# A vision block on one core: one loop for all heads in the transformer attention, f32 products by image and head triple, image blocks first, a mixture of experts in two phases

## The chip, the cores and the metric

The kernel runs on one core of a Trainium2 chip. A core has TensorE (PE in the rows; its loads of the stationary operand are shown apart as PEld), VectorE (DVE), ScalarE (ACT), GpSimd (POOL) and SyncE (SP), which only issues transfers here. The time is that of the device in microseconds; lower is better. Three runs of the kernel before took 524.59, 520.01 and 513.32 us, median 520.01. The execution that the profile shows took 514.25 us, of which 512.4 us are the span from the first instruction to the last.

## The reference

The input is 32 images as 36 patches of 768 numbers; all in all 1152 tokens of width 192.

```
h = x_patches @ W.T + b                                  # tokenizer: 1152 x 768 @ 768 x 192
xm, ref = h[:22], h[22:]                                 # 22 images, 10 reference images
m = 0.5 + 0.5*tanh(25*(c - 0.5)); c from cosines of a small gelu net of xm and ref
x = xm * m
3 times: q, v = x @ qv_w; attn = q k_ref' * s; attn = attn attn'; o = attn v (mean over refs)
         x = layernorm(x @ proj_w + proj_b, g, b)        # "diffuser"
h = layernorm(h + concat(m*x + (1-m)*xm, ref))
# transformer layer
x = h + softmax(q k' / 4) v @ proj_w + proj_b            # q, k, v of layernorm(h); 12 heads of 16,
                                                         # 36 tokens of one image attend to each other
xn = layernorm(x)
top 2 of 8 logits xn @ gate_w, softmax over the two
y = sum of the two experts: gelu(xn @ w1[e] + b1[e]) @ w2[e] + b2[e]     # 192 -> 768 -> 192
out = layernorm(h + x + y)
```

## The kernel before, in words

Tokens are worked on in 11 blocks of three images (108 rows, NT = 11); the last holds 72. Blocks 0 to 7 hold images of the diffuser (MT = 8; the last of them also holds the first references). Each engine has its own program, written out by hand as Python loops, and the order within it is the order of the text; semaphores (`S[...]`) tie the engines together. Nothing is scheduled by a planner. The stages are:

- **Tokenizer** (time 5 to 37 us). Per block six f32 matmuls, the bias by DVE (L955), two transposes (L400), a copy by ACT.
- **Prologue** (37 to 70 us). With all blocks there: the small net (three gelu passes), the reference keys, their Gram matrix, the cosines, the mask. ACT also issues here the nine transfers that fill the sort buffer `srt_dram` in memory with zeros (L746), ahead of the copies of the keys (L753).
- **Diffuser.** NI = 24 steps (three rounds of eight blocks) in a software pipeline: step i makes the queries and values of block i (`wq`, `wqv`), the products `rm` of step i-1, and the projection (`wpa`) of step i-5, whose result went through memory (`scratch`) to change its layout. Five more turns, 24 to 28, drain the pipeline. Beside this, ACT and POOL split 27 pieces of weights into a 16-bit high part (L731) and a bf16 low part (L1286): 24 for the experts, three for attention. Up to two pieces come in a turn, one on most; the last at turn 26. SP issues every transfer, in order.
- **Attention** (17 turns, about 220 to 369 us). A block passes through a pipeline of turns: features q and k as split products (three 16-bit matmuls for one f32 product), scores over the 108 x 108 tokens of three images with a barrier value between images, maximum by DVE (L1099), exponential by ACT (L850, one for each head), 12 transposes (L584), a split of the probabilities, 36 matmuls of 17 columns for the heads, a projection as a split product, residual sum, layer norm (statistics on DVE, the root on POOL by `pow`, L1261), logits, top 2, rank within the expert. Blocks go in the order 0 to 10, so that block 0 has to wait for the drained diffuser.
- **Routing.** Once all blocks are chosen, DVE makes a table of 25 tiles of 128 rows (L1162 to L1187); rows go to the sorted buffer by indirect transfers (L1291) and come back by tile (L366).
- **Mixture** (389 to 489 us). 25 tiles, each of 36 + 18 split products, a gelu in three pieces (ACT L901), a cast and a subtraction in two pieces (DVE L1206, L1208). POOL writes the scaled diagonals `dg` here (L1332).
- **End.** The results are read back by token, summed by PE with the diagonals of the gates, normed and stored.

The helpers `mm` (L395) and `turn` (L400) record nearly all matmuls and transposes, so these are told apart by the names of their operands.

## Time and profile before

| what | us |
|---|---|
| median of 3 runs (513.32 to 524.59) | 520.01 |
| profiled execution | 514.25 |
| its span | 512.4 |
| PE busy | 401.5 (78%) |
| DVE, POOL, ACT busy | 288.8, 233.3, 227.5 |
| mean granted clock of TensorE | 0.817 of 2.4 GHz |

A busy PE is not a PE at its peak: a matmul's end is modelled, and at the lower clock level (0.5, that is 1.2 GHz) the same work is busy for nearly twice as long. One f32 matmul is two records.

### The profile page before, as it was taken

The page shows a single profiled execution, that of the slowest core. Times are in us where ns is not written, and L with a number is a line of the kernel's source. Part 1 is how long each engine was busy: PE and PEld are TensorE (multiplying, and loading weights), DVE is VectorE, ACT ScalarE, POOL GpSimd, SP SyncE. Part 2 cuts the span into 40 slices and gives each one's busy share as a digit, 9 for nine tenths or more (in the row PEclk, how much of TensorE's full clock was granted, in tenths as well). Part 3 has the DMA queues.
Part 4 walks back from the last instruction along what each step waited for, and adds up shares of the span by engine and source line. Part 5 has one row for each costly group of instructions (what it writes and reads, how often), then busy time and mean ns, then how long its engine had stood idle before and what let it go on. Part 6 is the DMA issues. An engine that isn't in the chain of part 4 may idle for free.

```text
span 512.4 us, 12626 instructions
## 1 busy us (share of the span) xinstructions
PE 401.5 (78%) x4370; PEld 341.2 (67%) x4370; DVE 288.8 (56%) x843; ACT 227.5 (44%) x636; POOL 233.3 (46%) x358
## 2 busy tenths in 40 slices
PE   3996376889999965276999889876407999999974
PEld 3984354546766644175889789766406998989964
DVE  1111132234545567568988687653553888888823
ACT  1121313467777753157775555441104544445403
POOL 1000001366666656835475644435432666666524
PEclk9999567979999995559897676655556999999988
DMA  8706915447566652000000000000253776667233
GB/s 255 264 0 222 297 41 115 111 91 193 141 146 147 146 105 59 0 3 1 3 3 3 14 16 14 14 14 28 63 224 109 267 256 229 246 227 281 98 103 106
DMA packets 59725, 59.62 MB, mean 116 GB/s; under 512 B 36843, under 2 KB 46197, under 8 KB 58896
## 3 DMA queue, kind: packets, MB, share of 16 engines
q1 hardware_dynamic: 56400, 48.10, 31.3%
q10 hardware_dynamic: 1008, 7.15, 4.3%
q0 software_dynamic: 2256, 3.57, 2.2%
q8 instruction: 37, 0.61, 0.5%
q14 instruction: 24, 0.20, 0.1%
HBM read 25.55 MB, written 14.33 MB: 78 GB/s over the span
## 4 chain that ended last, share of the span: by engine, by line
PE 61%; DVE 11%; issue 6%; POOL 6%; ACT 5%; DMA 4%; ACTq 3%; SPq 3%; POOLq 0%; DVEq 0%
PE wide L395 27%; PE bank L395 27%; PE bank L400 4%; ACTq L746 3%; ACT xT L850 3%; PE bank L584 1%; POOL rstd L1261 1%; DVE xs L1017 1%; PE bank L660 1%; DMA bdm<-in_bdm 1%; PE wide L584 1%; DMA xT<-in_w 1%; DVE xT L1132 1%; POOL srt_dram L1291 1%; SPq L313 1%
## 5 line engine op out<-in xcount | busy, mean ns | idle before, releaser
L395 PEld LDWEIGHTS bank<-xT 108*32 108x32 f32 (+4 forms) x629 | 24.3, 144 | 36.7 <-issue 24.6
L395 PE MATMUL bank<-xT 108*32 108x96 f32 (+4 forms) x629 | 32.4, 263 | 19.5 <-ACT xT L731 11.4
L764 ACT ACTIVATE xT<-bank,gains 96x128 f32<-96x128 f32 (+1 forms) x72 | 29.0, 461 | 36.0 <-PE bank L660 36.0
L1291 POOL DMA_INDIRECT srt_dram<-row,dst x22 | 22.9, 1039 | 45.3 <-DVE dst L1089 39.6
L1337 POOL DMA_INDIRECT y_dram<-qkbm,ydst x25 | 26.0, 1038 | 35.7 <-DVE ydst L1214 27.1
L731 ACT ACTIVATE xT<-wide 108x288 f32<-108x288 f32 (+1 forms) x70 | 26.2, 410 | 35.9 <-PE wide L395 19.7
L395 PE MATMUL bank<-wqv,xTs 128*108 128x384 f32 x96 | 38.7, 529 | 4.4 <-DVE xT L1032 4.3
L1286 POOL TENSOR_TENSOR wqkl<-xT,wqkh 96x768 bf16<-96x768 f32 x2 | 3.2, 1632 | 84.9 <-ACT wqkh L731 84.9
L395 PE MATMUL wide<-xT 108*108 108x17 f16 (+4 forms) x511 | 39.4, 223 | 0.0
L395 PE MATMUL wide<-w2h,xs 128*128 x300 | 39.1, 246 | 0.0
L395 PEld LDWEIGHTS wide<-xT 108*108 108x108 f16 (+4 forms) x511 | 37.2, 161 | 0.0
L395 PE MATMUL wide<-w2l,xs 128*128 x150 | 36.9, 246 | 0.0
L1208 DVE TENSOR_TENSOR xs<-xT,xs 128x384 bf16<-128x384 f32 x50 | 35.4, 709 | 1.7
L1206 DVE CAST xs<-xT 128x384 f16<-128x384 f32 x50 | 28.8, 577 | 11.3 <-ACT xT L901 9.9
L850 ACT ACTIVATE xT<-bank,nmax 108x108 f32<-108x108 f32 x99 | 25.1, 369 | 22.7 <-DVE nmax L1099 22.7
L395 PE MATMUL bank<-tokw,xT 128*108 128x192 f32 x132 | 28.2, 372 | 8.0 <-DMA xT<-in_xT 5.3
L395 PE MATMUL wide<-xT,wqkh 96*128 96x108 f16 (+1 forms) x264 | 30.1, 261 | 4.2 <-DVE xT L1053 4.2
L1260 POOL TENSOR_SCALAR veps<-mv 108x1 f32<-108x1 f32 x46 | 10.8, 235 | 48.9 <-DVE mv L934 48.3
L395 PE MATMUL bank<-wpa,ocT 128*108 128x192 f32 x96 | 25.1, 391 | 7.3 <-DVE yb L1029 4.8
L395 PEld LDWEIGHTS bank<-tokw,xT 128*108 128x108 f32 x132 | 24.8, 202 | 9.0 <-DMA tokw<-in_tokw 5.2
L395 PEld LDWEIGHTS wide<-xT,wqkh 96*128 96x128 f16 x264 | 26.7, 128 | 4.8 <-ACT xT L731 3.8
L395 PE MATMUL wide<-xT,wqkl 96*128 96x108 f16 x132 | 29.3, 261 | 0.0
(257 smaller groups left out, 1240.2 us busy)
## 6 DMA issues: line engine op xcount, KB each, us to landing
srt_dram<-row ACTq DMA_DIRECT2D x8, 800.2 KB, 10.4
xT<-in_xT SPq DMA_DIRECT2D x11, 324.0 KB
tokw<-w1h SPq DMA_DIRECT2D x9, 384.0 KB
e1T<-w1l SPq DMA_DIRECT2D x9, 384.0 KB
hT<-in_w SPq DMA_DIRECT2D x8, 384.0 KB, 3.5
xT<-in_w SPq DMA_DIRECT2D x8, 384.0 KB, 3.6
vecs<-w1h SPq DMA_DIRECT2D x8, 384.0 KB
wqv<-w1l SPq DMA_DIRECT2D x8, 384.0 KB
```

The lines of the kernel that those rows point to most:

```text
L395: return nc.tensor.matmul(o, l, r, start=start, stop=stop)
L400: last = nc.tensor.transpose(o[:, f, :], i[:, f * HF:(f + 1) * HF], ident[0:T, 0:T])
L584: last = nc.tensor.transpose(bank[1 + r][0:T, g * T:(g + 1) * T], prob[:, 3 * r + g, :], ident[0:T, 0:T])
L731: return nc.scalar.activation(o, i, ACT.Copy)
L746: nc.scalar.dma_start(srt_dram[z * 96:(z + n) * 96].rearrange("(p r) w -> p (r w)", p=96), blank[:, 0:n * W]).then_inc(S["zeroed"], 16)
L764: last = nc.scalar.activation(o[:, f], i[:, f], ACT.Identity, scale=gains[:, which, 0, f:f + 1], bias=gains[:, which, 1, f:f + 1])
L850: last = nc.scalar.activation(prob[:, hh, :], bank[1 + r][0:T, g * T:(g + 1) * T], ACT.Exp, bias=nmax[:, hh:hh + 1])
L1206: V.tensor_copy(high, hidf[:, i % 2, cols]).then_inc(S["hidh_ready"], 1)
L1208: V.tensor_tensor(hidl[:, i % 2, o].rearrange("p j n -> p (j n)"), hidf[:, i % 2, cols], high, ALU.subtract).then_inc(S["hidl_ready"], 1)
L1260: link(G.tensor_scalar(ve, var, EPS, None, ALU.add))
L1291: G.indirect_dma_start(srt_dram, bass.IndirectOffsetOnAxis(dst[:, t, k:k + 1], 0), row[:, t, 0:W], None, bounds_check=EXP * CAP - 1, oob_i ...
L1337: G.indirect_dma_start(y_dram, bass.IndirectOffsetOnAxis(ydst[:, q:q + 1], 0), ysb[:, q % YB], None, bounds_check=2 * NTOK - 1, oob_is_err ...
```

## The change

What it does, by stage:

- **Tokenizer and prologue are one loop** (`for s in range(NT + 2)`). The reference blocks 7 to 10 come first (`TILES`), and the net, the keys, the Gram matrix and the mask of the first three blocks are worked out between the matmuls of later blocks. Only two constants (`FIRST`) are awaited ahead of the second block. The square root of the norms goes to POOL by `pow`. The zero fill is issued by SP, behind the inputs.
- **Diffuser.** The 24 steps stay. Attention has no more pieces to split; the 24 pieces of the experts are dealt two to a step in steps 0 to 4, one each in 5 to 10 and 14 to 21. The first layer norm of the three blocks of references alone (`begun`) stands in steps 11 to 13. The last five turns are inside the attention loop.
- **Attention** is one loop of 11 turns. All its products are f32. The order of blocks is `ATT` = 8, 9, 10, 0 to 7. DVE spreads the queries of a block into block-diagonal form by head triple (`qbd`, 108 columns: three heads of 36 tokens), so that scores are 12 matmuls of 36 columns against the 36 keys of one image, on 64 rows each. The probabilities are 108 x 432; maximum, addition and exponential are one instruction each; four transposes; four matmuls of 147 columns with values masked by image (`vj`), whose last columns give the sums; DVE masks and scales (`om`), and six matmuls with `dup` give the columns for the projection. Biases ride on a row of ones. ACT applies the layer norms.
- **Routing is spread** over the turns: block a is chosen in turn a+3 and its rows are sent at once.
- **Mixture in two phases.** Out of the first eight blocks of `ATT` come at least FULL = 5 full tiles. Their table is made in turn 10, and these tiles start while blocks 8 to 10 of the order go through the rest of attention and routing. The table of the other 20 tiles is made by DVE beside tile 2.
- **ACT** takes from DVE the cast of the hidden layer's high part (both halves in tiles 0 to 4, the second half afterwards), and from POOL the diagonals of the gates, in tiles 8 to 18. `RING` is 4 in place of 8.

```diff
+TILES = [*range(MT - 1, NT), *range(MT - 1)]
-RING, YB = 8, 3
+RING, YB = 4, 3
+AHEAD = 3
+SOON = NT - 3
+REFS_AT = NT
+ATT = [*range(MT, NT), *range(MT)]
+FULL = (2 * sum(min(T, B * N - t * T) for t in ATT[:SOON]) - EXP * (P - 1)) // P
...
-            return 3 + q // 2 if q < 6 else q
+            return q // 2 if q < 10 else q - 5 if q < 16 else q - 2
...
+            sp.wait_ge(S["zeros_ready"], 1)
+            blank = row[0:96].rearrange("p t w -> p (t w)")
+            for z, n in ZEROS:
+                sp.dma_start(srt_dram[z * 96:(z + n) * 96].rearrange("(p r) w -> p (r w)", p=96),
+                             blank[:, 0:n * W]).then_inc(S["zeroed"], 16)
...
+            sp.wait_ge(S["place_ready"], 1)
+            sp.wait_ge(S["row_stored"], 16 * 2 * SOON)
+            sorted_rows(0)
+            sorted_rows(1)
+            sp.wait_ge(S["exp_ready"], 1)
+            expert_weights(0)
+            expert_weights(1)
+            sorted_rows(2)
+            expert_weights(2)
             for i in range(WB, NTILE):
+                if i == FULL:
+                    sp.wait_ge(S["place_ready"], 2)
+                    sp.wait_ge(S["row_stored2"], 16 * 2 * (NT - SOON))
                 sorted_rows(i)
...
-                    for g in range(3):
-                        for r in range(4):
-                            rows = slice(32 * r, 32 * r + 32)
-                            last = split_mm(bank[1 + r][0:T, g * T:(g + 1) * T], [(qkh[rows, 0, g], qkl[rows, 0, g])],
-                                            [(qkh[rows, 1, g], qkl[rows, 1, g])])
+                    for u in range(2):
+                        for j in range(JB):
+                            for a in range(2):
+                                rows = slice(64 * a, 64 * a + 64)
+                                last = mm(wide[0:T, a, (u * JB + j) * N:(u * JB + j + 1) * N], qbd[rows, u, j], kT[rows, u, j * N:(j + 1) * N])
...
+            def mixed(a):
+                pe.wait_ge(S["pT_ready"], a + 1)
+                pe.wait_ge(S["av_ready"], a + 1)
+                pe.wait_ge(S["y_read"], min(NI - 4 + a, NI))
+                if a >= 1:
+                    pe.wait_ge(S["om_ready"], a)
+                for g in range(HG):
+                    last = mm(wide[0:T, 2 + g // 2, g % 2 * OG:g % 2 * OG + VW], pT[:, g * T:(g + 1) * T], vj[:, a % 2, g, :])
+                last.then_inc(S["ao_psum"], 1)
...
+            def high_of(i, a):
+                act.wait_ge(S["hid_ready"], HJ // 2 * i + 2 + a)
...
+                copy(hidh[:, i % 2, 3 * a:3 * a + 3].rearrange("p j n -> p (j n)"),
+                     hidf[:, i % 2, a * 3 * P:(a + 1) * 3 * P]).then_inc(S["hidh2_ready" if a else "hidh_ready"], 1)
```

How this moves instructions, at three places. First ACT, from the prologue to the first diffuser step. Before (`e1T` is the net's gelu, `srt_dram<-row` the zero fill, the copies `xT<-bank` behind it the reference keys, `th` the mask, `xTs` the transposed block):

```order
L742 ACTIVATE e1T<-wide,fc1b 48x432 x2
L742 ACTIVATE e1T<-wide,fc1b 48x324
L746 DMA srt_dram<-row 96x2134 x8
L746 DMA srt_dram<-row 96x1552
L753 ACTIVATE xT<-bank,rowm 108x192
L731 ACTIVATE xT<-bank 108x192 x3
L757 ACT_TABLE_LOAD
L757 ACTIVATE nrm<-nrm 108x11
L759 ACT_TABLE_LOAD
L759 ACTIVATE th<-cosm 108x8
L731 ACTIVATE xTs<-bank 96x216 x2
```

Now, from the fifth block on (the keys go to `xs`):

```order
L870 ACTIVATE e1T<-wide,fc1b 48x108
L854 ACTIVATE hT<-bank 96x2x108
L878 ACTIVATE xs<-bank 108x192
...
L854 ACTIVATE hT<-bank 96x2x108
L864 ACTIVATE th<-cosm 108x3
L870 ACTIVATE e1T<-wide,fc1b 48x108
L854 ACTIVATE xTs<-bank 96x216 x2
L943 ACTIVATE h<-h,mask 108x192
L854 ACTIVATE w1h<-xT 128x768
```

The nine transfers have left ACT, the keys are copied between the blocks, and no table is loaded between the last gelu and the mask.

Second PE, one turn of attention. Before, from the head products of a block to those of the next (`xT<-` 108x17 are the heads, 108x108 the scores, `wqkh`/`wqkl` the features, the L584 rows the transposes of the probabilities):

```order
L395 MATMUL wide<-xT 108x17 x36
L395 MATMUL wide<-wvph,xT 108x192
L395 MATMUL wide<-wvpl,xT 108x192
...
L395 MATMUL bank<-xT 108x108 x9
L395 MATMUL wide<-xT 108x108 x3
...
L395 MATMUL wide<-xT,wqkh 128x108 x2
L395 MATMUL wide<-xT,wqkl 128x108
...
L584 MATMUL bank<-ident,xT 108x108 x9
L584 MATMUL wide<-ident,xT 108x108 x3
```

Now one turn from turn 5 on, with its waits (108x147 are the heads, 108x36 the scores, `amask` is `dup`):

```order
L433 MATMUL bank<-xTs,wqk 128x108 [waits aq_ready,aoT_ready,qT_ready,x1T_ready]
L433 MATMUL bank<-xTs,wqk 128x108 x3
L641 MATMUL bank<-ident,xT 108x108 [waits taken_ready,pT_ready,p_ready]
L641 MATMUL bank<-ident,xT 108x108 x3
...
L433 MATMUL wide<-xT 108x147 [waits y_read,om_ready,av_ready,pT_ready]
L433 MATMUL wide<-xT 108x147 x3
L433 MATMUL wide<-xT 108x36 [waits e_ready,o_ready,res_ready,ak_ready,aq_ready]
L433 MATMUL wide<-xT 108x36 x11
...
L433 MATMUL bank<-amask,xT 96x36 [waits aoT_ready,aq_ready,om_ready]
L433 MATMUL bank<-amask,xT 96x36 x5
...
L433 MATMUL wide<-wvo,xT 108x192 [waits res_ready,e_ready,aoT_ready]
```

The 36 + 36 + 36 split matmuls of features, scores and heads are 8 + 12 + 4 of f32, 12 transposes are 4, and six matmuls are new.

Third PE, where the mixture starts (L750 are the transposes of sorted rows, `row` those of a block's router rows):

```order
L750 MATMUL bank<-ident,xT 96x128 [waits srt_in0,chosen_ready]
L750 MATMUL bank<-ident,xT 96x128
L438 MATMUL bank<-ident,row 96x108 [waits xn_ready]
L438 MATMUL bank<-ident,row 96x108
L433 MATMUL wide<-chosen,rank 108x8 [waits chosen_ready,e_ready]
L433 MATMUL wide<-chosen,rank 128x8
```

The rows of tile 0 are transposed here before the last three blocks have their ranks; before, tile 0 stood behind all of them.

## Rows read from the trace of the kernel before

**Rows 1.** The page's granted clock in 40 slices of 12.8 us, in tenths.

```profile
PEclk9999567979999995559897676655556999999988
```

**Rows 2.** Windows by stage: from:to, us, busy of each engine, granted clock, DMA share, GB/s.

```profile
104.00:177.00 73.00, 72.01 (x693) 49.11 (x694) 35.94 (x97) 51.84 (x133) 48.86 (x65) 0.96 0.63 145
233.00:354.00 121.00, 106.28 (x1428) 97.17 (x1428) 90.84 (x302) 68.75 (x239) 60.53 (x116) 0.73 0.04 10
354.00:387.00 33.00, 8.86 (x42) 7.58 (x42) 15.16 (x75) 2.86 (x8) 13.53 (x17) 0.50 0.37 126
387.00:489.00 102.00, 97.93 (x1394) 93.19 (x1395) 83.31 (x199) 49.55 (x126) 60.80 (x70) 0.97 0.59 212
```

**Rows 3.** Timeline, tokenizer and prologue: start, us, engine, line, operation, [idle before, releaser].

```profile
12.19 4.18 PE L395 MATMUL bank<-tokw,xT 128*108 128x192 f32 x12 [2.76 <-DMA bdm<-in_bdm]
34.46 2.12 PE L395 MATMUL bank<-tokw,xT 128*108 128x192 f32 x12
41.59 15.10 ACTq L746 DMA_DIRECT2D srt_dram<-row  x9
69.61 1.65 PE L395 MATMUL bank<-xTs,wq 128*96 128x108 f32 x8
```

**Rows 4.** Timeline, diffuser steps and their drained end.

```profile
101.20 0.84 ACT L731 ACTIVATE w1h<-xT 128x768 f16<-128x768 f32 x1 [4.27 <-DMA xT<-in_w]
177.30 0.91 PE L395 MATMUL bank<-xTs,wq 128*96 128x108 f32 x8
182.85 0.91 PE L395 MATMUL bank<-xTs,wq 128*96 128x108 f32 x8
190.84 2.05 DVE L1017 TENSOR_TENSOR xs<-xs,vecs 108x192 f32<-108x192 f32 x1 [1.94 <-ACT xs L782]
```

**Rows 5.** Timeline, first of the maxima of attention turns 0, 2, 4 and 10.

```profile
226.49 1.30 DVE L1099 TENSOR_REDUCE nmax<-bank 108x3 f32<-108x324 f32 x3 [0.62 <-PE wide L395]
243.47 1.29 DVE L1099 TENSOR_REDUCE nmax<-bank 108x3 f32<-108x324 f32 x3
260.33 1.28 DVE L1099 TENSOR_REDUCE nmax<-bank 108x3 f32<-108x324 f32 x3
332.41 1.29 DVE L1099 TENSOR_REDUCE nmax<-bank 108x3 f32<-108x324 f32 x3
```

**Rows 6.** Timeline, matmuls at either clock level.

```profile
262.39 1.33 PE L584 MATMUL bank<-ident,xT 108*108 108x108 f32 x9
265.01 0.46 PE L395 MATMUL wide<-gate,hT 96*108 96x8 f32 x4
287.41 0.76 PE L395 MATMUL wide<-gate,hT 96*108 96x8 f32 x4
171.12 0.90 PE L395 MATMUL bank<-wpa,ocT 128*108 128x192 f32 x4
171.95 0.63 PE L395 MATMUL wide<-rm,xT 32*108 32x96 f32 x12
```

**Rows 7.** Groups by form, whole span: line, engine, operation, shapes, count, busy, mean ns, idle.

```profile
L850 ACT ACTIVATE xT<-wide,nmax 108x108 f32<-108x108 f32 x33 | 9.8, 415 | 0.0
L782 ACT ACTIVATE xs<-yb,shift,rstd 108x192 f32<-108x192 f32 x24 | 13.1, 547 | 33.4 <-POOL shift L1264 33.3
L764 ACT ACTIVATE xTs<-bank,gains 96x108 f32<-96x108 f32 x32 | 12.3, 443 | 0.0
L1206 DVE CAST xs<-xT 128x384 f16<-128x384 f32 x50 | 28.8, 577 | 11.3 <-ACT xT L901 9.9 <-issue 1.3
```

**Rows 8.** Chain of waits, routing and first tile: start, us, what.

```profile
384.01 2.19 DMA xT<-srt_dram
389.05 2.72 PE bank L395 x24
```

**Rows 9.** Timeline, the last sending of rows, and PE's first matmul behind the mixture.

```profile
376.13 0.99 POOL L1291 DMA_INDIRECT srt_dram<-row,dst  x1 [0.30 <-issue]
489.34 1.48 PE L395 MATMUL bank<-h,ident 108*108 108x192 f32 x8
```

1535 lines of the change are left out of this document (870 added, 665 removed).

## The prediction

> **What bounds the kernel now.** I read the windows by stage first, then the timeline at the seams between stages. PE is the bound in two stages and in neither of the others. In the steady diffuser PE is busy for 72.01 of 73 us, in the mixture for 97.93 of 102 [rows 2]; the change leaves the work of both on PE as it is. In attention it is busy for 106.28 of 121 us, but at a granted clock of 0.73 [rows 1, 2], that is partly at 1.2 and partly at 2.4 GHz. In routing it is busy for 8.86 of 33 us: a chain of small instructions and waits. So what can be won lies in the prologue, at the drained end of the diffuser, in attention and in routing, and each is read at its seams: the diffuser's first `wq` at 69.61, its last at 182.85, the first maximum at 226.49, the one of turn 10 at 332.41, the first hidden matmul at 389.05, the first matmul behind the mixture at 489.34 [rows 3, 4, 5, 8, 9]. The sum goes from seam to seam against the profiled execution: 512.4 us of span and 1.85 around it, 514.25. The median of the runs shown is 520.01, 1.1% above it, and the three spread over 2.2%, so that the forecast for a median has a percent of doubt from there alone.
>
> **Tokenizer and prologue, new end 51 (before 69.61).** Block 1 started at 12.19 because its matmuls stood behind all early constants (2.76 us idle) [rows 3]. Now only two are ahead of it; the others are some 570 KB, and at the 245 GB/s of this stretch 2 us: start at about 10.5. A block's six matmuls take 2.12 us at the full clock and 4.18 at the low one [rows 3]; ten blocks 21, and 3 for the ramp of the clock as before. Between them PE now also does, per block, two transposes, two gelu matmuls of 108 columns and one of 24, and altogether eight key matmuls, sixteen of the Gram and `wqg` kind and four for the cosines. The nearest rows are eight records of 108 columns in 0.91 us and four of 8 columns in 0.46 [rows 4, 6]: a record is 0.09 to 0.1 us. That makes about 1.0 us a block, 11 in all, and 5 for the rest. 10.5 + 21 + 3 + 16 = 50.5, so 51. It replaces 32 us between the tokenizer's last matmul (34.46 + 2.12) and 69.61, of which 15.1 were ACT issuing the zero fill with the keys behind it [rows 3]. SP issues the fill now, while nothing behind it in its queue is due for another 15 us: at nothing, and if the fill held back the first pieces, their wait (as below) would cost about 4.
>
> **Diffuser, new last `wq` at 161 (before 182.85).** A steady step is 4.39 us, and 17 of them with one stall of 1.1 us led up to 182.85; so the sixth step began at 107 and the first six took 37.5 us, 11 more than steady. Part of that was ACT standing for pieces (4.27 us idle for one) with the step's copies behind them [rows 4]. Now two pieces come in each of steps 0 to 4, loaded a step ahead, the second behind the copies; but ACT also has the second half of the mask and a table load. I take half the excess off and a little back: 33 for the first six. Then 17 × 4.39 = 75, and 2 for the three double roots on POOL in steps 11 to 13. 51 + 33 + 75 + 2 = 161. That the second half of the late steps has no pieces on POOL also ends stalls such as the 2.05 us of DVE's multiplication at 190.84 [rows 4].
>
> **The seam to attention, new first maximum at 172.5 (before 226.49).** Before, 43.6 us lay between the last `wq` and the first maximum: five drained turns at the low clock and the split of attention's first block. Now the first attention block is a reference block that waits for nothing, and the drained turns lie within the loop. What is left is a step (4.4) and the features, the last products and the scores of turn 0, about 7: 11.5. Turns 0 to 4 carry one transposition, projection, bias, moments and normalisation each, priced below.
>
> **Attention, ten periods of 12.1 us (before 105.9 us, 10.6 each).** At the full clock two periods took 260.33 - 243.47, 8.43 each; the mean over ten is 1.26 times that [rows 5]. The new PE work of a turn, at the full clock: features 16 records 1.8 (eight are 0.91 [rows 4]); four transposes 0.6 (nine are 1.33 [rows 6]); values and projection 0.9 each (four records of 192 columns [rows 6]); heads eight records of 147 columns 1.0; six `dup` products, 12 records, 1.2 (four records are 0.46 [rows 6]); four transposes of 96 rows 0.7; logits and ranks 0.8. Scores have no row of their own: 24 records of 36 columns on alternate halves of the rows. One bound is 1.2 us (12 records on three row groups are 0.63 [rows 6]), the other 2.4 (no overlap, 0.1 each). I take 1.2, since the alternation is of the former kind. The sum is 9.1 and, with ends that overlap the next group taken off, 8.3; in turns 0 to 4 about 0.5 more. At the low clock the same rows are 1.65 to 1.8 times as long (0.76 for 0.46, 1.65 for 0.91 [rows 3, 4, 6]): 15.
>
> Here a rule can be laid beside the rows. At the low clock four short f32 records go from 0.46 to 0.76 us [rows 6]. The Trainium skill (TensorE: Matmul & The Clock Gate, LDWEIGHTS) puts a load of P columns at P / 1.2 ns, whatever the clock, 90 ns here. By it the 36 short records would not slow down, and a low-clock turn would be about 2 us shorter; the sum would be 435. The measured records decide. A rule against the change: the same skill (FP8 and Floating Point Precision, TensorE Precision Notes) has true FP32 in four passes, where the split products take three. By that alone the features, values and projection would cost 1 us more a turn, and attention would lose 10 us; the dropped transposes and the merged heads are what the rows set against it.
>
> A turn has a chain too. From ACT's copy of the keys to the next one: four row norms of 0.55, three masked copies of the values at 0.4, the heads' copy 0.35, the exponential over 432 columns (0.415 at 108 [rows 7]; I take 0.65), two affine copies 0.8: 5.2 us. Then PE's queries 0.9, transposes 0.6, ACT's copy 0.6, keys and their copy: 8.0, and with ten handoffs of 0.15 to 0.2 us 9.6. The chain is thus a little above PE's sum at the full clock, and below it at the low one. Between turns at either level I take the mix of before: 9.6 × 1.26 = 12.1. The bounds are 9.6 and 15. New maximum of turn 10: 172.5 + 121 = 293.5. So attention itself is forecast to be no faster than before, rather slower; the gain is in what lies around it.
>
> **Routing, new first hidden matmul at 309.5, 16 us later (before 56.6).** Before, 12.9 us went by from the last sending of rows (376.13) through the transfer (384.01) to 389.05 [rows 8, 9]; in front lay six more turns and a table. Now the eighth block is ranked in turn 10 itself: maximum and sum 1.3, `send_to` 1.2, POOL's two sendings 2.3, the way of before 12 from there, less 1 as the table is no longer ahead of it. About 16. DVE's 18 table instructions stand ahead of block 9's residual; 3.7 us, hidden by that transfer.
>
> **Mixture and end.** The work on PE stays: 489.34 - 389.05 = 100.3. Added: the last three blocks' residual, norm, logits and ranks between tiles 0 to 2, where PE, DVE and ACT wait for each other. I take 6 for these and 3 for two table loads around ACT's exponential in tile 5. The half of a cast that ACT takes over is about 0.55 us (DVE's was 0.577 [rows 7]); two of them, 0.8 for the columns and 1.15 for three gelus are 3.1 of a tile's 3.93, and 3.3 with the diagonals but one cast. At nothing, covered by PE; if ACT became the bound it would be 0.3 × 20 = 6. The end is 23.1 as before.
>
> **Sum.** 309.5 + 100.3 + 9 + 23.1 + 1.85 = 443.7, so **443 us**, 14% under the profiled execution.
>
> **The rivals.**
> - *Full clock.* The clock was 0.97 in the mixture and 0.96 in the steady diffuser [rows 2]; f32 products stream for longer. Then a turn is its chain, 9.6: 443 - 25 = 418. Against it: the chain leaves PE idle for 1.3 us of each turn, and before, at the full clock, PE was as dense and still lost it.
> - *Low clock throughout.* Before, from turn 6 on most slices show 0.5 to 0.7 [rows 1]. Then a turn is 15: 443 + 29 = 472.
> - *The two phases don't start early.* SP's queue is in order, and tile 0 needs rows, table and pr_psum of the last block; if the first five tiles wait for the whole routing chain, or starve behind it, some 20 us come back: 463.
> - *Slower than before.* One mechanism: short f32 products with 108 stationary columns whose loads don't overlap, at the low clock, with ACT's chain not beside them but behind. Scores 4.3 in place of 2.3, `dup` products 2.4, and ACT's 5.2 us exposed: 15 + 2.3 + 5.2 = 22.5, and DVE's 1.3 us ahead of them: 24. Ten periods add 119: 562. It decides from a period of 20.5 us on. Against it: score products on several row groups do overlap in this trace [rows 6].
>
> **Chances.** Forecast case (430 to 457) 0.50; full clock 0.20; low clock 0.17; phases not early 0.10; slower 0.02; 0.01 for about no change. The range runs from the full-clock case with an early prologue to the low-clock case: 412 to 476, the likeliest case's own 430 to 457. A difference of 2% is about what a measurement of this kernel can tell from none; faster by more 0.97, within 0.01, slower 0.02.
>
> **What would show it.** The first `wq` near 51 with no zero fill on ACT; the step still 4.4; the first maximum 11 to 12 us behind the last `wq`; maxima 9.6 to 15 apart according to the granted clock; the first hidden matmul 16 behind the last maximum, before the last three blocks' ranks; tiles of 3.93 from tile 3 on. It would be wrong if turns were over 15 at the full clock, or tiles stretched by ACT.

## The result, and the profile after

The changed kernel took 409.89 us (median of four runs, 404.55 to 414.34) against 520.68 for the kernel before: a ratio of 0.786 with an interval of 0.761 to 0.811. A second measurement, of six runs beside eleven of the kernel before, gave 413.98 us and 0.798 (0.793 to 0.803). Both ratios go by the faster runs of each kernel, since some executions of either are a per cent or two slower at a lower granted clock. It is faster, by about the amount of the case "full clock" (418), not by that of the forecast (443); at 409.9 it lies two microseconds under the range of 412 to 476.

The profiled execution took 414.34 us, of which 412.5 are the span. The page's granted clock, which answers to [rows 1]:

```profile
PEclk9999988999999998669999699995989999999969
```

The digits of 5 that filled the drained diffuser and the routing of the kernel before are gone, but for one slice. Next the windows of the changed kernel, from:to, us, busy of PE, PEld, DVE, ACT and POOL, granted clock, DMA share, GB/s; they answer to [rows 2]:

```profile
89.00:160.00 71.00, 68.41 (x679) 47.69 (x675) 37.93 (x102) 48.38 (x129) 48.09 (x87) 0.99 0.47 95
174.67:269.55 94.88, 90.44 (x825) 83.33 (x826) 67.55 (x223) 51.93 (x136) 57.02 (x137) 0.93 0.07 23
269.55:284.00 14.45, 11.15 (x73) 10.14 (x74) 9.48 (x43) 7.67 (x18) 4.68 (x9) 0.78 0.27 98
284.00:388.52 104.52, 98.52 (x1410) 96.54 (x1411) 77.32 (x213) 69.95 (x179) 48.22 (x56) 0.97 0.63 225
```

The second row is attention from the first maximum to that of turn 10: ten periods in 94.9 us at a clock of 0.93, where 121 were forecast. The seams, from the timeline (start, us, engine, line, operation, what ended the wait before it); they answer to [rows 3, 4, 5, 9]:

```profile
52.21 1.60 PE L433 MATMUL bank<-xTs,wq 128*96 128x108 f32 x8
159.29 1.65 PE L433 MATMUL bank<-xTs,wq 128*96 128x108 f32 x8
174.67 0.61 DVE L1402 TENSOR_REDUCE nmax<-wide 108x12 f32<-108x432 f32 x1 [6.06 <-PE wide L433]
269.55 0.61 DVE L1402 TENSOR_REDUCE nmax<-wide 108x12 f32<-108x432 f32 x1
284.00 0.27 PE L433 MATMUL bank<-xh,tokw 128*128 128x128 f16 x1 [0.47 <-DMA e1T<-w1l]
388.52 1.48 PE L433 MATMUL bank<-h,ident 108*108 108x192 f32 x8
```

| from seam to seam | before | forecast | after |
|---|---|---|---|
| to the first `wq` | 69.6 | 51 | 52.2 |
| to the last `wq` | 113.2 | 110 | 107.1 |
| to the first maximum | 43.6 | 11.5 | 15.4 |
| ten periods of attention | 105.9 | 121 | 94.9 |
| to the first hidden matmul | 56.6 | 16 | 14.4 |
| to the first final matmul | 100.3 | 109.3 | 104.5 |
| to the end | 23.1 | 23.1 | 24.0 |

Six of the seven seams were within 5 us, and their errors cancel to -3.3. Attention alone was off by 26.1. So the question for the experiments was why a turn takes 9.5 us and not 12.1, and what the factor 1.26 of the kernel before had been. In a row of undisturbed turns the maxima stand 8.8 us apart:

```profile
234.33 0.61 DVE L1402 TENSOR_REDUCE nmax<-wide 108x12 f32<-108x432 f32 x1 [0.17 <-PE wide L433]
243.13 0.61 DVE L1402 TENSOR_REDUCE nmax<-wide 108x12 f32<-108x432 f32 x1
251.94 0.61 DVE L1402 TENSOR_REDUCE nmax<-wide 108x12 f32<-108x432 f32 x1
```

The window between the last two of them, at the full clock:

```profile
243.13:251.94 8.81, 8.55 (x85) 7.81 (x86) 6.49 (x24) 5.43 (x15) 6.44 (x16) 1.00 0.07 21
```

### The profile page after: what moved, and what is told of

It reads as the page before. It is cut to its first block, busy times and chain, and to the rows that moved or that the text cites. A ratio compares the mean times of both kernels' runs of the same rounds, so it can differ in the third digit from the quotient of the medians.

```text
span 412.5 us, 11162 instructions
## 1 busy us (share of the span) xinstructions
PE 373.7 (91%) x3714; PEld 320.6 (78%) x3714; DVE 230.3 (56%) x703; ACT 225.4 (55%) x574; POOL 196.9 (48%) x339
## 4 chain that ended last, share of the span: by engine, by line
PE 72%; POOL 6%; DVE 6%; issue 6%; DMA 4%; ACT 3%; SPq 1%; ACTq 0%; POOLq 0%; DVEq 0%
PE bank L433 38%; PE wide L433 28%; PE bank L438 4%; POOL rstd L1536 2%; ACT xTs L885 1%; DMA srt_dram<-row,dst 1%; PE bank L750 1%; DVE xT L1261 1%; DMA xT<-in_xT 1%; PE bank L641 1%; POOL shift L1539 1%; POOL srt_dram L1575 1%; DMA e1T<-w1l 1%; POOL veps L1535 1%; POOL veps L1545 1%
## 5 line engine op out<-in xcount | busy, mean ns | idle before, releaser
L1619 POOL DMA_INDIRECT y_dram<-ysb,ydst x25 | 24.8, 993 | 49.1 <-PE wide L433 18.3
L854 ACT ACTIVATE xT<-bank 108x192 f32<-108x192 f32 (+3 forms) x57 | 21.0, 368 | 30.5 <-PE bank L433 17.7
L433 PE MATMUL bank<-xTs,wqk 128*128 128x108 f32 x176 | 28.5, 313 | 4.7 <-ACT xTs L885 2.8
L433 PE MATMUL wide<-xT 64*108 64x36 f32 (+2 forms) x368 | 32.2, 283 | 0.2 <-ACT xT L854 0.2
L433 PEld LDWEIGHTS wide<-xT 64*108 64x108 f32 (+1 forms) x368 | 29.8, 185 | 2.7 <-issue 2.3
L1575 POOL DMA_INDIRECT srt_dram<-row,dst x22 | 23.1, 1049 | 17.7 <-DVE dst L1317 9.8
L433 PEld LDWEIGHTS bank<-xTs,wqk 128*128 128x128 f32 x176 | 25.0, 219 | 8.2 <-ACT xTs L885 6.0
L433 PEld LDWEIGHTS bank<-xT 108*32 108x32 f32 (+2 forms) x316 | 14.2, 122 | 17.7 <-issue 17.3
L1536 POOL TENSOR_TENSOR rstd<-veps,nhalf 108x1 f32<-108x1 f32 x46 | 26.1, 567 | 3.8
L885 ACT ACTIVATE xT<-bank,gains 96x128 f32<-96x128 f32 x50 | 20.0, 448 | 14.3 <-PE bank L750 14.3
L433 PEld LDWEIGHTS wide<-w2h,xs 128*128 128x128 f16 (+1 forms) x300 | 26.4, 98 | 0.0
L854 ACT ACTIVATE xT<-wide 108x288 f32<-108x288 f32 x48 | 16.9, 405 | 14.7 <-PE wide L433 14.5
```

Of the source, the lines that this page charges most:

```text
L433: return nc.tensor.matmul(o, l, r, start=start, stop=stop)
L854: return nc.scalar.activation(o, i, ACT.Copy)
L885: last = nc.scalar.activation(o[:, f], i[:, f], ACT.Identity, scale=gains[:, which, 0, f:f + 1], bias=gains[:, which, 1, f:f + 1])
L1536: last = G.tensor_tensor(rstd[0:rows, k], ve, nhalf[0:rows], ALU.pow)
L1575: G.indirect_dma_start(srt_dram, bass.IndirectOffsetOnAxis(dst[:, t, k:k + 1], 0), row[:, t, 0:W], None, bounds_check=EXP * CAP - 1, oob_i ...
L1619: G.indirect_dma_start(y_dram, bass.IndirectOffsetOnAxis(ydst[:, q:q + 1], 0), ysb[:, q % YB], None, bounds_check=2 * NTOK - 1, oob_is_err ...
```

## Experiments on the changed kernel: TensorE, the clock and the gaps

Times of the whole are single runs unless said otherwise, and they spread by some us. So I read attention in its own ten periods (from the first maximum to that of turn 10). In six profiles whose attention code is that of the changed kernel these took 92.6 to 97.0 us, so that a difference of 4 us is not told from none.

**Scores twice.**

```diff
-                    for u in range(2):
+                    for again in range(2):
+                        for u in range(2):
```

> In the changed kernel, ten periods between maxima took 94.9 us, the undisturbed ones 8.8 each, at a granted clock of 0.93; TensorE was busy for 90.6 of 95 us. Here the twelve score products of each turn are made twice (the first set is overwritten), 24 more f32 records of 36 columns. If TensorE bounds the turn, all that the second set takes is added; the first set's rows show 2.3 us: period 11.1, ten of them 118, the whole some 25 us longer. If the chain through ACT and DVE is the bound, as the prediction had it for the full clock (9.6 us against 8.3 of TensorE), the second set first fills slack and the ten periods grow by 10 us or less. Both theories of the clock leave it at 0.93 or above here, since the added work is f32 and leaves no gap.

Measured: 419.75 us, ten periods 99.7 in place of 94.9, and no dip in the clock (windows of this run):

```profile
172.00:271.70 99.70, 95.22 (x1065) 88.81 (x1066) 67.60 (x224) 53.23 (x136) 57.31 (x137) 1.00 0.07 22
```

The 2.3 us expected were a misreading: that row holds the 147-column products too. Two rows show the size of the added set. The first is the changed kernel, the second this run; both begin with the same products:

```profile
240.65 2.43 PE L433 MATMUL wide<-xT 108*108 108x147 f32 x32
```

```profile
237.74 3.57 PE L433 MATMUL wide<-xT 108*108 108x147 f32 x56
```

24 more records are 1.14 us, 11.4 in ten turns. Without its one long turn (13.2 in place of 8.8) the changed kernel would have had 90.5; this run's 99.7 are 9.2 more. So about 0.8 of what is added to TensorE shows. TensorE's idle time stays at 4.4 to 4.5 us in either window (94.88 less 90.44, 99.70 less 95.22), so the added work fills no slack: TensorE bounds the turn, with the chain through ACT and DVE close behind. The forecast had it the other way round: 8.3 for TensorE, 9.6 for the chain. TensorE's 8.8 less a wait of 0.2 is 8.6, the 8.3 were nearly right, and the chain was put too long.

**Short 16-bit products added.**

```diff
+                    for z in range(42):
+                        mm(wide[0:T, 0, 432:449], w2h[0:T, z % EXP, z % HJ, 0:T], w2h[0:T, z % EXP, z % HJ, 108:125])
```

> Ahead of each turn's scores stand 42 products of 17 columns with 16-bit operands, whose result nobody reads: of the same kind as the 36 that made the heads in the kernel before, and at the full clock about as long as the doubled scores of the run beside it (2.1 to 2.3 us a turn). Theory of gaps (the clock falls where TensorE is idle in between): no gap is added, so the clock stays at 0.93 and the ten periods take 95 + 22 = 117 us. Theory of kinds (short 16-bit products don't hold the clock, whatever the gaps): the clock of attention falls toward the 0.73 of before, and the ten periods take 135 us or more.

**A gap each turn.**

```diff
                     last.then_inc(S["s_psum"], 1)
+                    pe.wait_ge(S["e_ready"], i + 1)
```

> No work is added: in each turn TensorE waits behind the scores until DVE has taken the maximum and added it, 1.2 us and two handoffs, which makes a gap of about 1.5 us a turn, as large as the idle time per turn in attention of the kernel before (14.7 us in 121). Theory of gaps: the clock falls toward 0.73, and a period goes from 8.8 to 10.3 and then by the clock to 12 or more: ten periods 120 to 135. Theory of kinds: the clock stays at 0.9 or above, and the ten take 95 + 15 = 110. In the least case, that the gap only replaces other waits, nothing changes.

Measured: 458.34 and 454.21 us. The windows of ten periods, first of the run with short products, then of the run with the gap:

```profile
173.12:310.72 137.60, 136.67 (x1245) 132.55 (x1246) 69.30 (x223) 52.87 (x136) 56.91 (x137) 0.73 0.05 16
```

```profile
170.97:301.46 130.49, 113.15 (x824) 107.12 (x824) 69.52 (x223) 53.67 (x139) 56.59 (x137) 0.74 0.06 17
```

Each brought the clock down to the level of before, the first with TensorE hardly idle (136.67 of 137.60), the second without a single product added. Neither theory excludes the other: here the added short products and the added gaps are each enough, and the f32 work of the doubled scores kept 1.00. What it is in the short products is not shown, since the two sets differ in three things: 42 products of 17 columns in 16 bits against 24 records of 36 columns in f32. TensorE's idle time grew from 0.44 to 1.73 us a turn, and the turn by 3.6.

**GpSimd's sends later.** The one long turn of the changed kernel (221.12 to 234.33) has this behind it: ACT waited 2.63 us for a norm's shift by POOL, then TensorE stood for 1.22, and then came 8 us at 0.57. Timeline of ACT and PE, then a window, in the changed kernel:

```profile
221.81 0.55 ACT L971 ACTIVATE row<-xT,shift,rstd 108x192 f32<-108x192 f32 x1 [2.63 <-POOL shift L1539]
224.88 0.90 PE L433 MATMUL wide<-wvo,xT 128*108 128x192 f32 x4 [1.22 <-ACT xT L854]
```

```profile
226.00:234.00 8.00, 8.00 (x54) 7.68 (x56) 4.11 (x15) 2.78 (x7) 5.93 (x14) 0.57 0.03 9
```

```diff
-                if i + AHEAD >= NT:
+                if i == NT - 1:
                     send(i - 3)
...
-                if 3 <= i < NT - AHEAD:
-                    send(i - 3)
+                for a in {5: [0], 6: [1], 7: [2], 8: [3, 4], 9: [5, 6]}.get(i, []):
+                    send(a)
```

> The changed kernel, in which GpSimd sends rows in turns 5 to 10 and not from turn 3 on. In turns 3 and 4 it had three norms, a sum and two sends, 9.3 us of work without a pause, and ACT waited 2.6 us for it in turn 5; TensorE stood for 1.22 us, the clock fell to 0.57 for 8 us, and that period was 13.2 us in place of 8.8. If this was GpSimd's backlog, the long period goes, ten periods take 88 to 91 us at a clock near 1.0, and the whole gains 4 to 6 us. If the stall is of another origin it stays, and nothing is gained. The price: the last sends are 1 to 2 us later, and with them tile 0 perhaps.

Measured: 416.93 us. The long turn is gone (9.5 us in its place), so GpSimd's backlog was its cause. But another of 13.0 us stands at the end (252.1 to 265.1); the ten periods are 94.6, and the seam to the first hidden matmul is 17.3 in place of 14.4, at a clock of 0.50. Ahead of the new stall ACT's copies begin 1.45 us behind TensorE's last value product (250.49 + 0.90), and then TensorE stands for 1.67:

```profile
250.49 0.90 PE L433 MATMUL bank<-wvo,xTs 128*108 128x192 f32 x4
252.84 1.05 ACT L1038 ACTIVATE xT<-bank,rowm 108x192 f32<-108x192 f32 x3 [3.73 <-PE bank L433]
254.83 0.90 PE L433 MATMUL wide<-wvo,xT 128*108 128x192 f32 x4 [1.67 <-ACT xT L854]
```

GpSimd issues its four sends in just this time (248.50 to 253.45), but no wait in the program ties ACT's copies to them. So this stall stands beside the doubled sends and is not shown to come from them; moving the sends gained nothing.

## Experiments on the kernel before: what the factor 1.26 was

**Filled with f32 work, and f32 products for the heads.**

```diff
                         if a == 1:
+                            for z in range(5):
+                                last = mm(bank[6][0:T, 3 * T:4 * T], ident[0:T, 0:T], ident[0:T, 0:T])
```

> The kernel before, with five f32 transpose-sized products of 108 columns (into columns that nobody reads) behind the key features of every attention turn: 1.1 us of f32 work at the full clock, where TensorE would then have waited for the exponential. Theory of gaps: with the longest wait filled the clock of attention rises from 0.73 to 0.85 or more, and ten periods take 105.9 or less, down to 98, although there is more work. Theory of kinds: most of a turn's records are still short 16-bit ones, the clock stays near 0.73, and the ten periods take 105.9 + 10 to 15 = 116 to 121.

```diff
-                    for hh in range(HEADS):
-                        last = split_mm(bank[7][0:T, hh * (HD + 1):(hh + 1) * (HD + 1)], ...
+                    for hh in range(8):
+                        last = mm(bank[7][0:T, hh % 2 * 102:(hh % 2 + 1) * 102], rank[:, 1, 0:T], prob[:, hh, 0:102])
```

> The kernel before, in which the 36 short 16-bit products that make the heads of a block (17 columns each, 1.93 us a turn at the full clock) are left out and eight f32 products of 102 columns stand in their place (sixteen records, about 1.8 us at the full clock); so the heads are not those of the reference, the order, the waits and the length of the work are the same. Theory of kinds: the clock of attention rises from 0.77 to 0.9 or more and ten periods fall from 105.9 us to 85 to 95. Theory of gaps: nothing about the gaps has changed, the clock stays at 0.77 and the ten take 103 to 108.

Both together:

> Both edits of the kernel before at once: f32 products in place of the 36 short 16-bit ones of the heads (so the heads are not those of the reference), and the five f32 products of 108 columns behind the features. Each alone left the clock of attention at 0.82 and 0.79, with TensorE idle for 15% and 8% of it. If idle time and short products each hold the clock down, and both must go, it rises here to 0.9 or more, and ten periods take 93 to 98 us, less than the 105.9 of before although each turn has 1.1 us more work. If the clock hangs on something else (the order of stages, the chain through DVE), it stays at 0.8 and the ten take 108 to 115.

Measured: 521.64, 516.29 and 517.21 us (the kernel before 513.77, 516.35 and 512.59 beside them); ten periods 111.8, 108.1 and 106.6 at clocks of 0.79, 0.82 and 0.89. The first lies between its two expectations, the second near that of gaps, and the third is in neither: with both edits the clock rose by 0.12, and the ten periods were not shorter. Nearly 35 us of that last run, its last three turns, show why (window):

```profile
301.60:336.10 34.50, 28.48 (x375) 24.49 (x372) 24.84 (x93) 20.73 (x72) 16.68 (x24) 0.95 0.06 17
```

At a clock of 0.95 the turns are still 11.5 us long, and TensorE is idle for 6 of 34.5. Nor is it the added work that makes them long. The five added products lie in a wait: the transposes behind them still wait 0.23 us for ACT three times a turn. The f32 head products take 1.74 us at the full clock where the short ones took 1.95; in the middle turn of the three, where the clock dipped (0.57 from 318 to 322), they took 2.95:

```profile
318.23 2.95 PE L395 MATMUL wide<-xT,rank 108*108 108x102 f32 x16
330.63 1.74 PE L395 MATMUL wide<-xT,rank 108*108 108x102 f32 x16
```

The other two turns had the full clock throughout and took 11.2 and 10.8 us (windows):

```profile
301.61:312.82 11.21, 9.21 (x135) 7.99 (x132) 8.70 (x33) 7.26 (x25) 5.58 (x8) 1.00 0.06 18
325.30:336.05 10.75, 8.15 (x109) 6.67 (x105) 7.94 (x31) 6.22 (x22) 5.56 (x8) 1.00 0.06 17
```

So the late turns of the kernel before had another bound for the most part, and I formed a new theory: a ring (maxima, exponentials, transposes, heads, DVE's splits and choice, maxima).

**DVE's order changed.**

```diff
                 (behind the maxima of turn i)
+                if 0 <= i - 6 < NT:
+                    choose(i - 6)
+                if 0 <= i - 7 < NT:
+                    send_to(i - 7)
```

> The kernel before, with DVE's choice of experts and its rank arithmetic (twelve small instructions, 2.1 us) behind the next block's maxima and no longer ahead of them. In the run with both fillings the last three turns of attention had a clock of 0.95 and still took 11.5 us each, against 8.4 in the first turns, where no block is routed yet. Theory of the ring: from turn 5 on a turn is a ring (maxima, exponentials, transposes, heads, DVE's choice, maxima), and the low clock comes with TensorE's waits in it. Then the late turns lose the 2.1 us at least, down to 9.5 to 10.3 from 12.0, ten periods take 92 to 98 in place of 105.9, and the clock rises from 0.77 to 0.85 or more. Theory of the clock alone: DVE's order matters little; ten periods stay at 103 or more.

Measured: 518.42 us, ten periods 109.1, clock 0.72. It decides nothing, since the edit made a wait of its own: GpSimd's sends came ahead of the root on which DVE waits, and TensorE waits for DVE.

```profile
320.36 0.96 DVE L940 TENSOR_SCALAR row<-yb,mv,rstd 108x192 f32<-108x192 f32 x1 [2.06 <-POOL rstd L1262]
```

> The run with DVE's choice behind the maxima said nothing clear: with it GpSimd's two sends came to stand ahead of the norm's root, DVE waited 2.06 us for that root and TensorE 2.13 for DVE. Here the sends stand a turn later on GpSimd too, behind the root, so that the order of DVE is changed alone. Theory of the ring: the late turns of the kernel before come down from 12.0 us to 10.3 or less, ten periods to 92 to 98. Theory of the clock: the late turns keep 11.5 to 12, ten periods 103 or more.

> The same order, and both fillings of the kernel before (f32 products in place of the short ones of the heads, so that these are not the reference's, and five f32 products of 108 columns a turn). The fillings alone had raised the clock to 0.89, to 0.93 in the late turns, which kept 11.5 us. If ring and clock each held the late turns, only both edits free them: 9.3 us a turn, ten periods 93 to 96 at a clock of 0.95. If the choice is not what closes the ring, the late turns stay at 11.5 and the ten at 105.

Measured: 501.51 and 500.52 us (the kernel before 512.86 beside them); ten periods 99.5 at a clock of 0.79 and 97.3 at 0.96. The order alone gave 6.4 us of attention at nearly the same clock (0.77 before), nearly all of it in the three turns from 260.33 to 296.56, which took 36.2 before and 30.8 now. In the four runs with the old order these three turns took 36.2 to 39.0, so this is more than their spread. With both fillings at work the order is worth more: the same three turns take 38.5 without it and 28.3 with it. The last three turns gained nothing (35.8 before). First with the order alone, then with all three edits (windows):

```profile
288.20:323.80 35.60, 33.89 (x442) 31.53 (x440) 26.67 (x93) 21.19 (x72) 20.52 (x30) 0.70 0.07 19
```

```profile
285.20:320.70 35.50, 29.31 (x412) 26.43 (x410) 26.43 (x92) 21.18 (x72) 20.56 (x30) 0.95 0.07 19
```

35.6 us at a clock of 0.70 and 35.5 at 0.95: here the clock is worth nothing. By the rows it is GpSimd's sends that close these turns. The last send and the maxima behind it, first with the order alone, then with all three edits:

```profile
310.45 0.99 POOL L1292 DMA_INDIRECT srt_dram<-row,dst  x1 [0.31 <-issue]
311.94 1.30 DVE L1099 TENSOR_REDUCE nmax<-bank 108x3 f32<-108x324 f32 x3 [1.09 <-remote]
```

```profile
307.40 1.05 POOL L1294 DMA_INDIRECT srt_dram<-row,dst  x1 [0.31 <-issue]
308.89 1.30 DVE L1101 TENSOR_REDUCE nmax<-bank 108x3 f32<-108x324 f32 x3 [1.04 <-remote]
```

In both runs the maxima of each of the last three turns start 0.44 to 0.50 us behind the end of GpSimd's second send. From the maxima to the moments on DVE it is 5.0 us, from there through GpSimd's root, differences, sums and sends 6.3, and 0.5 more to the next maxima: 11.8, a turn, and no TensorE work lies in it. The program has no wait of the maxima for the sends, and the profile puts the end of the wait to no engine; why DVE stands there is open. And this ring comes with the edit: in the kernel before the sends ended 8.0 us or more ahead of the maxima. So for its late turns only the run with both fillings speaks.

Ten periods at the 8.43 us of the two fast ones [rows 5] would be 84.3; the kernel before had 105.9. An estimate for the 21.6 between, from the rows above: the three middle turns lost 10.9 to that pace, of which DVE's order gave back 5.4 and 3.0 are left even with it at a clock of 1.00 (28.3 less 25.3); the last three lost 10.6, of which 7.0 to 8.3 are left in turns of 10.8 to 11.2 us at the full clock. That is 15 to 17 us for waits. 5 to 6 are left for the clock, about a quarter of what I had put on it.

## Experiments on the other terms

**The drained steps ahead of attention.** The five results are made before the loop on PE, ACT, DVE and POOL, and no longer in its turns 0 to 4:

```diff
+            for k in range(5):
+                turn_result(NI - 5 + k, NI)
...
+                projection(NI - 5 + k)
```

> The changed kernel with the last five steps' results (transposition, projection, bias, moments, normalisation) taken out of attention's turns 0 to 4 and made ahead of the loop, as in the kernel before. They are a chain of about 3 us each there (two transposes 0.35, ACT's copy, projection 0.9, bias, and the next), so the first maximum comes 15 us later, and the five turns give back 1.6 us of TensorE's each, 8 in all: +5 to +9 us. If a sparse stretch ahead of attention decides about its clock, there is more: ten periods at 0.75 in place of 0.93 to 1.0, 115 us or more, +25 to +30 in all.

Measured: 426.35 us. The seam to the first maximum is 27.2 in place of 15.4, the ten periods 91.6 in place of 94.9, at the same 0.93: +8.5 by these two, inside the range (the whole is 12.0 above the profiled execution, the rest lies in other seams). The 3.3 us that the turns gave back are less than the 8 expected, and no more than profiles of one code differ by. A sparse stretch ahead of it does not decide about attention's clock. Of the 28.2 us that this seam lost, 11.8 are the folding; the rest I put on the order of blocks and what no longer has to be split, by subtraction: no run takes these apart.

**One phase.**

```diff
             sp.wait_ge(S["row_stored"], 16 * 2 * SOON)
+            sp.wait_ge(S["row_stored2"], 16 * 2 * (NT - SOON))
             sorted_rows(0)
```

with the ranks of the last three blocks and the second table ahead of tile 0 on each engine.

> The changed kernel without its early phase: all eleven blocks are ranked and sent, and both tables made, before the first tile's rows are fetched. In the changed kernel the first hidden product comes 14.4 us behind turn 10's maximum. The three last blocks' routing (a residual, a norm, a transposition, logits and ranks that wait for each other, about 4 us for each that no other work hides), the table of 20 tiles (3.7) and the transfer (8) then stand ahead of it: 30 to 34 us behind that maximum, and the mixture gets back the 4 us that it took more than before. So +12 to +16 us. If the early phase's worth is mainly that TensorE's clock doesn't fall, the mixture's first tiles show it too (+3 more). If it were hidden anyway: within 4 us of the changed kernel.

Measured: 427.28 us. The routing seam is 35.2 us in place of 14.4, the mixture 98.4 in place of 104.5: the early phase is worth 14.7 by these two seams (12.9 by the whole). The rest of the 42.2 us that the routing seam lost I put on spreading, by subtraction; no run shows it alone.

**The zero fill back on ACT.**

```diff
+            for z, n in ZEROS:
+                nc.scalar.dma_start(srt_dram[z * 96:(z + n) * 96]...
             from_turn(0)
```

> The changed kernel with the eight transfers of zeros issued by ACT behind the tokenizer's loop, ahead of the first diffuser block's columns, as before they stood ahead of the keys. An issue took ACT 1.7 us before (15.1 for nine), most of it while the inputs still came. If the price of an issue is in its queue's room, and room is short only while inputs come, eight issues cost about 0.1 to 0.4 each here: +1 to +3 us at the first query product. If the price is fixed by the 800 KB that each moves, the first query product comes 13 to 15 us later, and the whole is 13 to 15 us longer.

Measured: 428.11 us, the first `wq` at 66.98. The issues (eight of 800 KB and a smaller one), first on SP in the changed kernel, then on ACT in this run:

```profile
16.76 4.39 SPq L348 DMA_DIRECT2D srt_dram<-row  x9
```

```profile
50.91 15.17 ACTq L1004 DMA_DIRECT2D srt_dram<-row  x9
```

The same transfers cost SP 4.4 us, right behind the issues of all inputs, and ACT 15.2 at a time when SP issues only first pieces of weights: the price is not the room that the inputs take. The first `wq` comes 14.8 us later, and the whole is 13.8 above the profiled execution.

**The casts back on DVE.**

```diff
-                if i >= FULL and a == 0:
-                    V.tensor_copy(high, hidf[:, i % 2, cols]).then_inc(S["hidh_ready"], 1)
+                V.tensor_copy(high, hidf[:, i % 2, cols]).then_inc(S["hidh2_ready" if a else "hidh_ready"], 1)
```

> The changed kernel with both halves of the hidden layer's cast on DVE in all tiles, as before; ACT makes none. The prediction put the move to ACT at nothing, covered by TensorE, whose work of a tile is 3.7 to 3.9 us: the time from the first to the last hidden product stays within 2 us of 104.5. The other side: DVE's work of a tile (casts 0.58 each, subtractions 0.73 each, bias 0.36, high part 0.29, destinations 0.4) then comes to 3.7 us, and with its handoffs it, not TensorE, sets the tile: 0.1 to 0.3 us more on each of 25, +3 to +7.

Measured: 416.61 us. Tiles by their results' bias, first the changed kernel, then this run:

```profile
350.26 0.35 DVE L1497 TENSOR_TENSOR ysb<-wide,hT 128x192 f32<-128x192 f32 x1
353.94 0.35 DVE L1497 TENSOR_TENSOR ysb<-wide,hT 128x192 f32<-128x192 f32 x1
357.60 0.34 DVE L1497 TENSOR_TENSOR ysb<-wide,hT 128x192 f32<-128x192 f32 x1
```

```profile
352.07 0.35 DVE L1493 TENSOR_TENSOR ysb<-wide,hT 128x192 f32<-128x192 f32 x1
355.95 0.35 DVE L1493 TENSOR_TENSOR ysb<-wide,hT 128x192 f32<-128x192 f32 x1
359.83 0.35 DVE L1493 TENSOR_TENSOR ysb<-wide,hT 128x192 f32<-128x192 f32 x1
```

3.67 us a tile with ACT's casts in this stretch (in other profiles 3.6 and 4.0 in turn), 3.88 without, and the kernel before had 3.9. Over 14 tiles in the middle of the mixture the mean is 3.95 here and 3.77 to 3.83 in four profiles of the unchanged mixture. So the move that I put at nothing gave 0.1 to 0.2 us a tile, 2 to 4 in all. That DVE, not TensorE, set the tile before is argued from this, and fits the other side of the expectation; no wait of TensorE in the profile shows it. The mixture took 109.0 in place of 104.5, but with unchanged code it took 109.7 in another profile: the period of a tile shows this, the sum doesn't.

**Products of zeros at the start and the end; the gates' exponential by a power.**

```diff
+            for z in range(14):
+                mm(bank[7][0:T, 0:P], warm[0:T, 0:T], warm[0:T], False, False)
             for t in range(NT):
```

> The changed kernel with products of a zero tile at two places: eight ahead of the tokenizer (TensorE is idle there until 5.17 us and its first two blocks take 4.15 us each in place of 2.12) and fourteen between the start of the final sums and the arrival of the expert results (3.4 us idle, after which sixteen records take 5.42 us in place of 2.9). Theory of gaps: the first two blocks take 2.1 to 3 us each and the final sums come 2 us earlier; the whole gains 2 us at the end, and at the start up to 3, unless the tokenizer waits for its inputs anyway (DMA at 98% of its time up to 38 us), which I expect: -2 us in all. If the products don't move the clock: the end is later by the little that they overlap, 0 to +1.

```diff
-                    nc.scalar.activation(vv[:, 1, :], vv[:, 0, :], ACT.Exp).then_inc(S["gex_ready"], 1)
...
+                    link(G.memset(vv[:, 1, :], 2.718281828459045))
+                    G.tensor_tensor(vv[:, 1, :], vv[:, 1, :], vv[:, 0, :], ALU.pow).then_inc(S["gex_ready"], 1)
```

> The changed kernel with the exponential of the gates made by GpSimd as e to a power, so that ACT loads no table in the mixture. The prediction put 3 us on the two loads in tile 5 (1.28 each and their place in the gelus). Tile 5's period was 5.7 us in the changed kernel, the others' 3.7 to 4.0. If the loads are the cause, it comes down to about 4: -1.7 to -2.5 us in all. If it is the fetch of rows behind the second table (the same tile is the first of it), it stays at 5.5 and nothing is gained.

Measured: 414.78 and 413.91 us. With the zeros the end takes 22.0 us in place of 24.0, as expected (23.2 to 25.1 in other profiles without them); at the start the first block takes 2.17 us in place of 4.15, and then the second waits for its input:

```profile
5.20 2.17 PE L434 MATMUL bank<-tokw,xT 128*108 128x192 f32 x12 [0.76 <-DMA xT<-in_xT]
9.56 3.09 PE L434 MATMUL bank<-tokw,xT 128*108 128x192 f32 x12 [2.19 <-DMA xT<-in_xT]
```

With the power the slow tile takes 4.5 us in place of 5.7: the two table loads were 1.2 of my 3.

**All three mends, beside the changed kernel on the same chip, six runs each.**

> The changed kernel with three edits: GpSimd's sends later (4 to 6 us if the backlog theory holds), the exponential of the gates by a power on GpSimd (1.4 us, as the run of it alone showed in tile 5), and products of zeros while TensorE waits for the expert results at the end (2 us). Sum: 7 to 9 us less than the changed kernel on the same chip, about 2%, some 400 us.

> The changed kernel itself, as the base for the run beside it: 405 to 415 us, ten periods of attention 95 us, one of them 13 us long, the seam from turn 10's maximum to the first hidden product 14.4.

Measured: 413.55 us (409.88 to 420.68), ratio to the kernel before 0.801 (0.794 to 0.807); the changed kernel 413.98 (409.09 to 417.05), 0.798 (0.793 to 0.803). No gain, where 7 to 9 us were expected. The sends gave back in a late turn of 13.0 us and in the routing seam (17.1) what they took from turn 6; the other two should leave 3 us, and such a difference is within what these runs can tell. The changed kernel stays the fastest that was run.

The profile of the changed kernel taken here met its expectation in the seam (14.4) but not in attention: the ten periods are 96.9, and the same wait of 2.63 us for GpSimd and the same stand of TensorE (1.23) are followed by two long turns, 14.4 and 12.5 us (window):

```profile
212.56:239.48 26.92, 25.61 (x177) 24.05 (x178) 14.59 (x50) 12.43 (x32) 16.27 (x35) 0.68 0.05 15
```

That is 9.3 us more than two turns of 8.8, where the first profile lost 4.4.

## Why the prediction was wrong

The direction was right, the number was 33 us too high. By its steps:

- **Tokenizer and prologue** (51; 52.2), with ACT's 15.1 us of issues on the path: right, and shown by putting them back. (Its 245 GB/s are 262 in the stretch from 5.28 to 12.19; that changes nothing.)
- **Diffuser** (110; 107.1): right in the sum, with one row misread. The `wq` that stands 17 steps ahead of 182.85 is at 100.09 and not at 107; between it and the next one lie 11.1 us, so that 6.7 of the 11 us in excess stood in one stall and not spread over the first steps:

```profile
100.09 0.91 PE L395 MATMUL bank<-xTs,wq 128*96 128x108 f32 x8
111.17 0.91 PE L395 MATMUL bank<-xTs,wq 128*96 128x108 f32 x8
```

- **Seam to attention** (11.5; 15.4): low by 4; I had priced the features and scores of turn 0 at the full clock, and the stretch has 0.72.
- **Attention** (121; 94.9): the failed step is "Between turns at either level I take the mix of before: 9.6 × 1.26 = 12.1". The factor is the ratio of all ten periods to two fast early ones of the kernel before, and I took it for the clock because the clock was low in the late turns (the two early ones, called full clock in the prediction, had 0.90, as the window below shows). The runs on the kernel before show that most of it was waits between the engines, of DVE's order above all: by the estimate above 15 to 17 of 21.6 us. And the changed kernel shows in its place a turn of 8.8 us at a clock of 1.00, set by TensorE. What is the clock's own can't be carried over either, since it fell with added gaps and with added short products, and the change alters both: in the changed kernel it falls behind a wait of 1.22 us, and costs 4.4 us in one profile and 9.3 in another. Then the two sums: TensorE 8.3 (measured 8.6), chain 9.6 (below 8.8, since TensorE binds). The two early periods of the kernel before (window):

```profile
243.47:260.33 16.86, 15.49 (x270) 14.43 (x268) 15.58 (x45) 13.20 (x46) 8.95 (x21) 0.90 0.01 3
```

- **The two rules.** The rule of f32 in four passes (the Trainium skill, FP8 and Floating Point Precision, TensorE Precision Notes), by which a turn would cost 1 us more than with the split products, can't be seen: a full-clock turn is 8.8 us where it was 8.43 at a clock of 0.90, with fewer and longer products, and no run here shows passes apart. For short f32 products the trace shows 24 score records in 1.14 us at the full clock (above) and, in turn 0 at the low one, in 2.38, twice that:

```profile
172.25 2.38 PE L433 MATMUL wide<-xT 64*108 64x36 f32 x24
```

  The Trainium skill (TensorE: Matmul & The Clock Gate, LDWEIGHTS) has a load of P columns take P / 1.2 ns, with no condition on the clock, 90 ns for 108; an estimate from it is 2.2 us for the 24 in both cases. The low-clock row is near that, the full-clock one half of it; the measured rows decide, as in the prediction's sum.

- **Routing** (16; 14.4): right; the early phase is worth 14.7.
- **Mixture** (109.3; 104.5): the 9 for disturbed tiles and table loads came out as 4.2. The loads cost 1.2, not 3, and the casts by ACT gave 2 to 4 where I wrote nothing, because I took TensorE for the bound of the tile. In other profiles of this mixture the seam is 105.7 to 109.7, so that the 9 were less far off than this one shows.
- **The rivals.** "Full clock" was the case, at a chance of 0.20: 418 by a period of 9.6. That the measured mean of 9.49 meets it is in part luck: an undisturbed turn is 8.8, and the long one and the five with the diffuser's results fill the mean up. The case against it, that at the full clock TensorE was as dense before and still lost it, used the same mistaken reading (those two periods had a clock of 0.90). The range ended at 412, from this rival with an early prologue; it left out that the turn could be shorter than 9.6, though TensorE's sum of 8.3 stood beside it.

## What to carry to other kernels

When a stage's turns grow from its start to its end, look at what joins them (here routing on DVE, sends on GpSimd) before putting the growth on a clock that is low at the same time: a low clock can be the trace of a wait and not its cause. A factor read off one kernel is no property of the chip; price the new turn from its own sums, TensorE's and the chain's, and carry both the low and the full clock as cases. A late turn that keeps its length when the clock rises has another bound; look which engine's last instruction ends just ahead of it. And a wait of one microsecond on TensorE cost four here, and nine in another profile, so a queue that falls behind once (GpSimd with two sends and three norms in a turn) is worth more than its own idle time.

## What the runs showed of the hardware

- The same nine transfers of zeros cost the issuing engine 0.49 us each on SP and 1.69 on ACT. Why is open.
- The granted clock fell from 0.93 to 0.73 by 42 added products of 17 columns a turn although TensorE was busy for 99% of the time, and to 0.74 by 1.3 us more idle time a turn with no product added. With 24 more f32 records a turn it was 1.00.
- Two indirect sends by GpSimd, of about 1.05 us each, stood ahead of each late maximum on DVE in the two runs with DVE's new order: six maxima of six began 0.44 to 0.50 us behind the end of the second send, with no wait for it in the program. Why is open.
- In code that is alike, the clock can differ from run to run: the first four periods of the kernel before took 33.8 us at 0.90, and in the run with DVE's order changed, whose edit only begins in turn 6, 40.0 us at 0.67. What decides between them stays open.
